# Block 0: one row maximum ahead of the phase work and one behind it, a denser first phase, norms in halves

## What is computed

```python
for i in range(NL):                                  # 6 layers, 16 heads of 8 features
    xn = _adaln(x, noise_emb, n1_w[i], n1_b[i])      # layernorm, scale and shift by batch
    q, k, v = split(xn @ qkv_w[i].T)
    x = x + _attn(_rope(q), _rope(k), v, src_mask) @ so_w[i].T
    xn = _adaln(x, noise_emb, n2_w[i], n2_b[i])
    q = _rope(xn @ cq_w[i].T)                        # 56 queries a batch and head
    k, v = _rope(context @ ck_w[i].T), context @ cv_w[i].T     # 1500 keys
    x = x + _attn(q, k, v, ctx_mask) @ co_w[i].T
    xn = _adaln(x, noise_emb, n3_w[i], n3_b[i])
    x = x + gelu(xn @ f1_w[i].T + f1_b[i]) @ f2_w[i].T + f2_b[i]
```

## Time and profile before

| | |
|---|---|
| median of 3 runs | 6731.15 us (6730.87 to 6737.94) |
| the profiled execution's own time | 6731.41 us |
| its span, first to last instruction | 6729.6 us |
| mean granted TensorE clock | 0.944 |
| PE matmul busy | 6157.6 us, 92% |
| PE weight loads busy | 4423.3 us, 66% |
| VectorE (DVE) busy | 3932.6 us, 58% |
| ScalarE (ACT) busy | 3320.6 us, 49% |
| GpSimd (POOL) busy | 2243.1 us, 33% |
| chain that ended last | PE 68%, DVE 8%, POOL 7%, issue 6%, ACT 4% |

### The profile page before, as it was taken

One profiled execution on the slowest core, in us unless ns is written; L12 is line 12 of the kernel. 1 busy time (PEld: TensorE's weight loads), 2 busy tenths in 40 slices (PEclk: granted clock), 3 DMA queues, 4 the chain that ended last, 5 costly groups with the idle time before them and its releaser, 6 DMA issues.

```text
span 6729.6 us, 141162 instructions
## 1 busy us (share of the span) xinstructions
PE 6157.6 (92%) x56181; PEld 4423.3 (66%) x56181; DVE 3932.6 (58%) x8705; ACT 3320.6 (49%) x6385; POOL 2243.1 (33%) x2179
## 2 busy tenths in 40 slices
PE   5799999999999999999989999999679999989998
PEld 4466666666666666666653777777457777756983
DVE  2677777777777777777765334444434444444552
ACT  1466656666566665665654334444223333333763
POOL 3555555555555555555520000000011111137430
PEclk6799999999999999999989899999889999999988
DMA  1566656656566565665740110000010000021000
GB/s 47 89 101 94 104 90 104 101 92 105 90 102 105 88 106 91 101 105 91 109 83 7 24 37 28 28 34 23 13 28 10 15 15 10 15 79 36 2 3 20
DMA packets 396487, 407.88 MB, mean 61 GB/s; under 512 B 125575, under 2 KB 372946, under 8 KB 393786
## 3 DMA queue, kind: packets, MB, share of 16 engines
q1 hardware_dynamic: 395834, 398.85, 33.4%
HBM read 158.00 MB, written 0.46 MB: 24 GB/s over the span
## 4 chain that ended last, share of the span: by engine, by line
PE 68%; DVE 8%; POOL 7%; issue 6%; ACT 4%; DMA 2%; SPq 1%; POOLq 1%; DVEq 0%; ACTq 0%
PE psum L2205 10%; PE psum L2172 9%; PE psum L1546 6%; PE psum L1534 6%; PE psum L1520 6%; PE psum L1560 4%; PE psum L2217 4%; PE psum L1568 3%; PE psum L1666 3%; POOL slot_context L3369 2%; DVE row_max L1885 2%; PE psum L435 2%; PE psum L421 2%; PE psum L1675 1%; DMA key_stack<-key_parts 1%
## 5 line engine op out<-in xcount | busy, mean ns | idle before, releaser
L1885 DVE TENSOR_REDUCE row_max<-psum 112x1 f32<-112x500 f32 x2304 | 1443.7, 669 | 283.4 <-PE psum L1534 278.5
L2003 ACT ACTIVATE weights<-psum 125x448 f32<-125x448 f32 x2304 | 1154.8, 544 | 769.6 <-PE psum L1520 754.6
L1520 PEld LDWEIGHTS psum<-query_stack,key_stack 121*125 121x125 bf16 x9216 | 829.2, 140 | 368.4 <-issue 166.1
L1534 PE MATMUL psum<-key_stack,query_stack 97*112 97x500 bf16 x2304 | 905.5, 394 | 106.3 <-DVE row_max L1885 80.4
L1520 PE MATMUL psum<-query_stack,key_stack 121*125 121x112 bf16 x9216 | 931.3, 224 | 70.2 <-ACT weights L2003 65.0
L2737 POOL TENSOR_TENSOR l_ctx_v<-l_ctx_v,l_ctx_w 125x512 f32<-125x512 f32 x48 | 61.0, 1271 | 2257.2 <-DVE l_ctx_v L2731 2257.2
L2205 PE MATMUL psum<-l_ctx_v,l_turned 125*128 125x128 f32 x5376 | 713.6, 281 | 16.2 <-ACT l_turned L2243 12.4
L2285 DVE TENSOR_REDUCE l_stat<-psum 128x1 f32<-128x1500 f32 (+1 forms) x224 | 391.6, 1748 | 574.9 <-PE psum L2172 574.9
L2205 PEld LDWEIGHTS psum<-l_ctx_v,l_turned 125*128 125x128 f32 x5376 | 643.1, 191 | 58.8 <-ACT l_turned L2243 40.2
L1546 PE MATMUL psum<-weights,values 125*17 125x112 f32 x18432 | 678.4, 266 | 0.2 <-ACT weights L2003 0.2
L1546 PEld LDWEIGHTS psum<-weights,values 125*17 125x17 f32 x18432 | 379.5, 97 | 264.2 <-ACT weights L2003 146.9
(11 more groups left out here) (526 smaller groups left out, 10251.9 us busy)
## 6 DMA issues: line engine op xcount, KB each, us to landing
key_stack<-key_parts SPq DMA_DIRECT2D x1728, 125.0 KB, 4.5
ctx_t<-in_ctxT SPq DMA_DIRECT2D x96, 750.0 KB
l_ctx_v<-in_ctxV SPq DMA_DIRECT2D x32, 750.0 KB
query_stack<-query_parts SPq DMA_DIRECT2D x576, 28.0 KB, 3.7
l_ctx_t<-in_ctxT SPq DMA_DIRECT2D x16, 750.0 KB
slot_context<-in_ctxV SPq DMA_DIRECT2D x16, 750.0 KB
key_stack<-ctx_mask_rows SPq DMA_DIRECT2D x576, 3.9 KB
sm_w<-in_sm_w SPq DMA_DIRECT2D x3, 2048.0 KB
```

The lines of the kernel that those rows point to most:

```text
L1520: mm = e.matmul(self.k.psum[0:KN, h, (p % 4) * QC:(p % 4 + 1) * QC], ks[:, p, kt * KN:(kt + 1) * KN], q[:, p * QC:(p + 1) * QC])
L1534: e.matmul(self.k.psum[0:QC, 2 + n % 2, 0:500], q[0:ROWS_MAX, p * QC:(p + 1) * QC], ks[0:ROWS_MAX, p, c * 500:(c + 1) * 500]).then_inc(sel ...
L1885: e.tensor_reduce(self.largest[:, i % PAIRS, i // PAIRS:i // PAIRS + 1], k.psum[0:QC, 2 + i % 2, 0:500], AX.X, ALU.max, negate=True).then_ ...
L2003: e.activation(half(self.p[kt % 2], h), self.k.psum[0:KN, h, 0:HALF], ACT.Exp).then_inc(self.exped.sem, 1)
```

## The change

Four things. (1) In VectorE's step the order becomes: at kt 10 the maxima's parts; the first reduction; the phase work of step k-1; the second reduction; at kt 11 the row copy; the fixed work. (2) `T_SELF` becomes a function of the phase: in phase -1 the eight batches of the self attention start every 2 steps (t = 26, 28, ... 40), in all others as before. (3) The waits for the tables and for the ones move from ahead of the loops to the first instruction that needs them; GpSimd makes the masks at t = 23 of phase -1. (4) The norms work in halves of 448 tokens: four tiles of 112 tokens for each, with a square root, a reciprocal, a spread and the multiplications of their own.

```diff
@@ Block0.vector
-        e.wait_ge(self.ones_stacked.sem, self.ones_stacked())
-        e.wait_ge(self.tables_arrived.sem, self.tables_arrived())
         for s in self.slots():
             for kt in range(KT):
                 last = 12 * s + kt - 1
-                self.phase_vector(e, last // (12 * BH), last % (12 * BH))
+                found = self.max_at(s, kt)
                 if 0 <= s + 1 < NS and kt == 10:
                     self.max_parts_vector(e, s + 1)
+                if found:
+                    self.largest_vector(e, *found)
+                self.phase_vector(e, last // (12 * BH), last % (12 * BH))
+                if found:
+                    self.largest_vector(e, found[0], found[1] + 1)
                 if 0 <= s + 1 < NS and kt == 11:
                     self.rows_vector(e, s + 1)
-                if self.max_at(s, kt):
-                    b, n = self.max_at(s, kt)
-                    for i in range(n, n + 2):
-                        e.wait_ge(self.max_scored.sem, self.max_scored(b, i))
-                        e.tensor_reduce(...)
                 self.fixed_vector(e, s, kt)
+    def largest_vector(self, e, b, n):
+        e.wait_ge(self.max_scored.sem, self.max_scored(b, n))
+        e.tensor_reduce(self.largest[:, n % PAIRS, n // PAIRS:n // PAIRS + 1], self.k.psum[0:QC, 2 + n % 2, 0:500], AX.X,
+                        ALU.max, negate=True).then_inc(self.max_read.sem, 1)
@@ phase dates
-T_SELF = [26 + 9 * i // 2 for i in range(BH)]
+T_SELF = lambda ph: [26 + (2 * i if ph < 0 else 9 * i // 2) for i in range(BH)]
+T_MASKS = 23
@@ phase_vector, at the rotary work
+            if (ph, n) == (-1, 0):
+                e.wait_ge(self.tables_arrived.sem, self.tables_arrived())
@@ fixed_scalar, at the first key's high part
+            if n == 0:
+                e.wait_ge(self.ones_stacked.sem, self.ones_stacked())
@@ phase_scalar, at the first MLP
+            if (mlp, f) == (0, 0):
+                e.wait_ge(self.tables_arrived.sem, self.tables_arrived())
@@ gpsimd
-        e.wait_ge(self.tables_arrived.sem, self.tables_arrived())
-        e.tensor_scalar(self.src_mask, self.src_mask8, LOW, None, ALU.mult)
-        e.tensor_scalar(self.mask_rows, self.ctx_mask8, LOW, None, ALU.mult)
-        e.drain().then_inc(self.masks_ready.sem, 1)
         for s in self.slots():
             for kt in range(KT):
+                if 12 * (s % BH) + kt == T_MASKS and s < 0:
+                    e.wait_ge(self.tables_arrived.sem, self.tables_arrived())
+                    e.tensor_scalar(self.src_mask, self.src_mask8, LOW, None, ALU.mult)
+                    e.tensor_scalar(self.mask_rows, self.ctx_mask8, LOW, None, ALU.mult)
+                    e.drain().then_inc(self.masks_ready.sem, 1)
@@ ln_tensor
-    e.wait_ge(k.ln_square.sem, k.ln_square(n, 0))
-    for i in range(TT):
-        if i == 3:
-            e.wait_ge(k.ln_square.sem, k.ln_square(n, 1))
-        mm = e.matmul(k.psum[:, 4, i:i + 1], k.sq[:, i * 128:(i + 1) * 128], k.mean_w[:, 0:1])
-    mm.then_inc(k.ln_var.sem, 1)
-    e.wait_ge(k.ln_rstd.sem, k.ln_rstd(WHOLE(n)))
-    for i in range(TT):
-        mm = e.matmul(k.psum[:, 2 + i // 4, (i % 4) * 128:(i % 4 + 1) * 128],
-                      k.stats[:, TT + i:TT + i + 1].broadcast_to([128, 128]), k.ident[:, :])
...
+    for c in range(2):
+        e.wait_ge(k.ln_square.sem, k.ln_square(n, c))
+        for i in range(NQ):
+            mm = e.matmul(k.psum[0:ROW, 2 + c, i:i + 1], half(k.sq, c)[:, i * ROW:(i + 1) * ROW], k.mean_w[:, 0:1])
+        mm.then_inc(k.ln_var.sem, 1)
+    for c in range(2):
+        e.wait_ge(k.ln_rstd.sem, k.ln_rstd(WHOLE(n), c))
+        for i in range(NQ):
+            mm = e.matmul(k.psum[:, 2 + c, i * ROW:(i + 1) * ROW],
+                          k.stats[:, 2 + c, i:i + 1].broadcast_to([ROW, 128]), k.ident[0:ROW, 0:ROW])
+        mm.then_inc(k.ln_spread.sem, 1)
```

More of the change, by code:

```diff
@@ L13 @@
 HALF = T // 2
+ROW, NQ = 112, 4
 BH = B // 2
@@ L272, in ln_scalar @@
         e.activation(half(k.sq, c), half(k.dev, c), ACT.Square).then_inc(k.ln_square.sem, 1)
-    e.wait_ge(k.ln_var.sem, k.ln_var(WHOLE(n)))
-    e.activation(k.stats[:, 0:TT], k.psum[:, 4, 0:TT], ACT.Sqrt, bias=k.eps_col).then_inc(k.ln_std.sem, 1)
+    for c in range(2):
+        e.wait_ge(k.ln_var.sem, k.ln_var(WHOLE(n), c))
+        e.activation(k.stats[:, c, :], k.psum[0:ROW, 2 + c, 0:NQ], ACT.Sqrt, bias=k.eps_col[0:ROW, :]).then_inc(
+            k.ln_std.sem, 1)
 def ln_vector(e, k, n, src, dst, per_batch=None, per_feature=None):
@@ L281, in ln_vector @@
         e.tensor_tensor(half(k.dev, c), half(src, c), k.psum[:, c, 0:HALF], ALU.subtract).then_inc(k.ln_dev.sem, 1)
[L282 to L291, removed]
-            e.drain()
-            for c in range(2):
-                v = by_batch(half(dst, c))
-                g = per_batch[j][:, c * BH:(c + 1) * BH]
-                o = e.tensor_tensor(v, v, spread(g, S), op)
-                if j == 1:
-                    o.then_inc(k.ln_done.sem, 1)
-    if per_feature is not None:
-        e.drain()
-        for c in range(2):
-            v = half(dst, c)
-            e.tensor_scalar(v, v, per_feature[0], per_feature[1], ALU.mult, ALU.add).then_inc(k.ln_done.sem, 1)
+    for c in range(2):
+        e.wait_ge(k.ln_std.sem, k.ln_std(WHOLE(n), c))
+        e.reciprocal(k.stats[:, 2 + c, :], k.stats[:, c, :]).then_inc(k.ln_rstd.sem, 1)
+    for c in range(2):
+        v = half(dst, c)
+        e.wait_ge(k.ln_spread.sem, k.ln_spread(WHOLE(n), c))
+        op = e.tensor_tensor(v, half(k.dev, c), k.psum[:, 2 + c, 0:HALF], ALU.mult)
+        if per_batch is not None:
+            v = by_batch(v)
+            g, b = (spread(a[:, c * BH:(c + 1) * BH], S) for a in per_batch)
+            e.drain()
+            e.tensor_tensor(v, v, g, ALU.mult)
+            e.drain()
+            op = e.tensor_tensor(v, v, b, ALU.add)
+        if per_feature is not None:
+            e.drain()
+            op = e.tensor_scalar(v, v, per_feature[0], per_feature[1], ALU.mult, ALU.add)
+        op.then_inc(k.ln_done.sem, 1)
 def rows_tensor(e, k, n, src, m):
@@ L1397, in phase_order @@
         if nxt:
-            for i, a in enumerate(T_SELF):
+            for i, a in enumerate(T_SELF(ph)):
                 if t == a:
@@ L2084, in gpsimd @@
                         self.norm_gpsimd(e, name, ph, layer, t - at - 5)
-                for i, a in enumerate(T_SELF if NEXT_OF(ph) is not None else ()):
+                for i, a in enumerate(T_SELF(ph) if NEXT_OF(ph) is not None else ()):
                     if t == a - 1:
```

12 lines of the change are left out of this document (4 added, 8 removed).

## The result

The changed kernel takes **6858.57 us** in the median of four runs (6848.46 to 6876.73), the kernel before, beside it, 6731.07: a ratio of **1.019**, 95% interval 1.0167 to 1.0213. It is slower, as forecast, but by 127 us and not by 45, and above the range. The profiled execution took 6876.73 us (span 6874.9); it is the slowest of the four, so what its trace shows is some 18 us more than the median has.

What follows compares the result with a forecast made beforehand. PE was taken as the bound, a chain of steps with small holes. 6731.4 + 102 (order) - 18.7 (start) - 37 (first phase) - 2 (norms) = 6775.7, taken as 6776 us, 0.7% slower; range 6714 to 6815.

Steps and rivals of the forecast that it cites:

- order on VectorE: In the slots, later phase work and row copy delay PE by 9.0 us a phase, +102 us in all.
- start: At the kernel's start, VectorE's first deviation no longer waits for the ones: -18.7 us.
- dense first phase: Phase before the slots: a batch every 2 steps fills PE's waits, at full clock: -37 us, bounds -19 and -40.
- norms, and all else: Norms in halves: reciprocal waits go, extra passes cost, scaling overlaps the spread: -2 us, bounds -11 and +10.
- the one on the row copy: Slot ends: the copy behind both maxima delays the next slot's first score, 3.5 us a phase, partly covered by phase matmuls.
- All 9.0 us a phase: PE's delay in the slots: 6.1 for phase work plus 3.5 for the row copy, less 0.6 for the earlier parts.
- the two halves of the order: In the slots: phase work behind the first reduction, 6.1 us a phase; row copy behind both maxima, 3.5.
- The row at half clock: First phase: PE runs at 1.2 GHz even over 4.43 busy of 4.50 us; by it the dense phase gives -19.
- the slots' row: Slots: PE 94% busy at granted clock 0.97, taken as nearest to a dense first phase over 90% busy.
- the plain slot ends: At t = 83 and 95 the next slot starts 1.0 us later, 0.4 comes back, net 0.6.
- the place of the waits: In the slots, PE's wait for row maxima grows beyond 6.5 us a phase, at a step's second maximum.
- rival 1: In the slots PE swallows the order's delays: 6674 us, or 6714 with the row copy's loss kept; chance 0.14 together.

Runs made afterwards that it cites:

- undo_order: The changed kernel with VectorE's old order (phase work, parts, row copy, then both reductions), all else kept: 6694.07 us, ratio 0.9944.
- spaced_first: The changed kernel with VectorE's old order and the first phase's self attention batches 4.5 steps apart again: 6714.78 us, ratio 0.9975.
- The early release: The changed kernel with the transposed maxima copied from their PSUM bank to a small tile ahead of the first reduction, wide copy still late: 6800.08 us, ratio 1.0099.
- order_only: The kernel before with the new order on VectorE and nothing else: 6892.68 us, ratio 1.0242.

## Why the prediction was wrong

The direction was right, from the right mechanism: PE stops for phase work and row copy that VectorE does later. Term by term:

| term | predicted | measured | from |
|---|---|---|---|
| order on VectorE | +102 | +164.5 | changed kernel less `undo_order` |
| start | -18.7 | -18.4 | first score, 244.0 to 225.6 in `spaced_first` |
| dense first phase | -37 | -20.7 | `undo_order` less `spaced_first` |
| norms, and all else | -2 | +2 | what is left of the 127.5 |

1. **The step that failed is the one on the row copy: "at t = 23, 35 and 71 PE's phase matmuls cover it", and the 0.9 and 0.1 for t = 47 and 59.** I asked only who reads the copy's output, not what its input holds. The matmuls that were to cover it need its bank: at t = 35, 47 and 59 (L1662, L1687, L1675) they wait 3.2 us a phase, where the sum had 1.0. At t = 23 and 71 no such wait shows. At t = 11 the wait of the next slot's score grew by 2.0 us (0.48 to 2.46), where the sum had 1.3. The early release gave back 58 us, with what the clock lost behind these waits.

2. **The sum had no term for PE's clock behind a longer stop.** All 9.0 us a phase were idle time, and idle time grew by 10.2; matmuls at 1.2 GHz added 7.6. The kernel before already showed the effect: PE waits 2.35 us in step 19, and step 20 is at 0.58. I read the clock as one mean over the slots, 0.97, and took it for constant. The two errors are tied: the early release took 50 us off PE's busy time in the slots, as much as the new order had added (49). This is also where the 42 us sit by which the two halves of the order cost more together than apart: their idle time adds up, their busy time does not.

3. **The first phase: the wrong end was taken.** The row at half clock, from this very phase, gave -19, and -20.7 was measured; the slots' row was taken as the nearer and was not. By the rule that the prediction quoted (the Trainium skill, "TensorE: Matmul & The Clock Gate", Part 1: activity releases the throttle) the dense phase was to run fast; here it did not, with PE busy for 36.48 of 40 us at 0.50.

4. Right were the start (-18.4 for -18.7), the idle time of the two halves of the order (69 us for the phase work and, without the waits for the bank, 35 for the copy, where the sum had some 60 and 39), the plain slot ends, the place of the waits (the row maximum's grew from 6.5 to 7.3 us a phase and from 7 to 11 waits), and the order's price once bank and clock are taken out, 109 us for 102. That PE would swallow the delays (rival 1) was wrong.

5. The norms were not run alone, so their price is not shown. Behind the last score the changed kernel is 14.7 us shorter (3237.1, from 6874.9 - 3637.8, against 3251.8), but `order_only`, which has the old norms, is 10.0 shorter there too (3241.8, from 6900.7 - 3658.9), so most of that can't be put down to them. And with the old order the slots grew by 17.5 us (3251.3 in `undo_order`, 3233.8 before): most phases there take 276 to 277 us as before, two take 283, with PE busy for 265.16 us in one of them instead of 258.84. The +2 in the last line of the table is a sum of such pieces. What sets the clock back in these phases and not in the others stays open; it may also be why runs of the changed kernel spread more.

## What to carry to other kernels

When an instruction is moved back, list who waits for the buffer it reads, not only for the one it writes: the next user of a rotating bank may be unrelated work. A stop of PE costs its length and, where the granted clock falls behind it, part of the following matmuls again, so look at the clock step by step before costing a new wait; a few unneeded matmuls in a stop that can't be removed may be cheaper than the slow stretch behind it. Of two rows for an unknown price, the one from the stage that is changed was the better guide here.

## What was not expected of the hardware

In the first phase PE was busy for 36.24 of 40 us and still had a granted clock of 0.54; with 168 short bf16 matmuls added it was busy for 38.49 and had 0.93, and the phase ended 17.3 us sooner. In the slots the step behind a wait of 2.35 us ran at 0.58, and sixteen short matmuls inside that wait, 1.1 us in all, kept it at 1.00. The same stop did not cost the same in each phase: step 36 took 2.6 to 4.9 us in the changed kernel, with the same instructions.
